# |d| from the score's bank and logistic nodes in place of |tanh| nodes, and the fold's product moved behind R's, in an attention and expert kernel

## What is computed

```python
def _L0_conv_ref(x, Wf, bf, Wg, bg, Wh, bh, Wv, bv, gamma):    # self-attention in each image
    s = jnp.einsum('bnd,bmd->bnm', xf @ Wf + bf, xf @ Wg + bg)
    o = gamma * (jax.nn.softmax(s, axis=-1) @ (xf @ Wh + bh)) @ Wv + bv + xf

def step(carry, ht):                                           # _L1_attn_ref, scanned over 256 tokens
    H_prev, H_prev_tilde = carry                               # the last 5 tokens and outputs
    temp = jnp.tanh(H_prev @ W1 + (ht @ W2)[:, None, :] + H_prev_tilde @ W3)
    w_t = jax.nn.softmax(temp @ v, axis=1)
    ht_hat = jnp.sum(H_prev_tilde * w_t, axis=1)
    ht_tilde = ht + jax.nn.relu(ht_hat)
    ...                                                        # both windows move on by one

t = _to_tokens(x)
t = t + _L1_attn_ref(_ln_t(t), v, W1, W2, W3)
t = t + _L1_ffn_ref(_ln_t(t), Wr, br, W1, b1, W2, b2)          # top 2 of 8 experts, Gelu
```

## Time and profile before

| | |
|---|---|
| runs (us) | 582.26, 577.89, 580.36, median 580.36 |
| the profiled execution | 582.32 us, of which its span 580.40 |
| busy | PE 557.9 us (96%), PEld 446.0 (77%), DVE 413.3 (71%), ACT 354.0 (61%), POOL 47.4 (8%) |

### The profile page before, as it was taken

The page is one execution under the profiler, slowest core; times in us unless marked ns, Lnnn a source line. Parts: engine busy times, 40 slices in busy tenths (PEclk is TensorE's granted clock), DMA queues, the critical chain, the costliest instruction groups (busy, mean ns, idle before and its releaser), DMA issues. The chain is left out here.

```text
span 580.4 us, 19441 instructions
## 1 busy us (share of the span) xinstructions
PE 557.9 (96%) x6331; PEld 446.0 (77%) x6331; DVE 413.3 (71%) x2867; ACT 354.0 (61%) x1440; POOL 47.4 (8%) x101
## 2 busy tenths in 40 slices
PE   6999879999999999999999999999999999999987
PEld 3555436778888888888888888888888888888875
DVE  2456555777777878787877787878787877777763
ACT  2335645556666666666666666666666666666654
POOL 1000000010101010101010101010101010101010
PEclk9555569999999999999999999999999999999999
DMA  8000000000000000000000000000000000000000
GB/s 228 17 2 1 0 0 3 2 3 2 3 6 3 6 3 7 3 7 3 6 3 6 3 6 3 7 3 7 2 6 3 6 3 7 2 7 3 8 2 10
DMA packets 7507, 5.84 MB, mean 10 GB/s; under 512 B 1216, under 2 KB 6896, under 8 KB 7408
## 3 DMA queue, kind: packets, MB, share of 16 engines
q1 hardware_dynamic: 6784, 4.57, 2.8%
q10 hardware_dynamic: 528, 0.03, 0.1%
q0 software_dynamic: 96, 0.00, 0.0%
HBM read 3.55 MB, written 1.05 MB: 8 GB/s over the span
## 5 line engine op out<-in xcount | busy, mean ns | idle before, releaser
L470 ACT ACTIVATE th<-bank 128x32 f32<-128x32 f32 x255 | 51.3, 201 | 145.4 <-PE bank L696 145.4
L938 DVE TENSOR_TENSOR_SCAN CC<-th,DE 128x16 f32<-128x16 f32 x510 | 115.3, 226 | 0.5 <-issue 0.5
L728 PE MATMUL bank<-f,hid 128*128 128x128 f32 x512 | 112.9, 302 | 1.0 <-ACT hid L492 0.6
L497 ACT ACTIVATE GF<-Z,cst 64x32 f32<-64x32 f32 x255 | 105.4, 413 | 11.7 <-DVE Z L989 2.5
L942 DVE SCALAR_TENSOR_TENSOR DE<-CC,yh 128x40 f32<-128x40 f32 x509 | 81.9, 203 | 27.2 <-DVE yh L1005 0.5
L938 DVE TENSOR_TENSOR_SCAN C<-th,DE 128x16 f16<-128x16 f32 x255 | 49.3, 193 | 73.0 <-ACT th L470 68.3
L633 PE MATMUL bank<-xnT,f1p 128*128 128x128 f16 x1024 | 99.2, 219 | 0.2 <-ACT hid L492 0.2
L696 PE MATMUL bank<-Tf,v 128*128 128x32 f32 x510 | 99.3, 277 | 0.0
L685 PE MATMUL bank<-Tf,nv 128*128 128x32 f32 x510 | 98.9, 276 | 0.0
L492 ACT ACTIVATE hid<-bank,b1T 128x128 f32<-128x128 f32 x256 | 94.4, 369 | 5.7 <-PE bank L633 4.8
L694 PE MATMUL bank<-GF,cst 128*128 128x32 f32 x510 | 95.3, 269 | 0.0
(11 more groups left out here) (135 smaller groups left out, 827.3 us busy)
## 6 DMA issues: line engine op xcount, KB each, us to landing
x_tok<-in_x_dram SPq DMA_DIRECT2D x4, 256.0 KB, 4.3
f<-in_L_ffn_W_dram SPq DMA_DIRECT2D x1, 1024.0 KB
out_dram<-acc SPq DMA_DIRECT2D x16, 64.0 KB
w<-in_L_attn_W_dram SPq DMA_DIRECT2D x3, 64.0 KB, 3.9
cst<-shape_constants_dram SPq DMA_DIRECT2D x1, 148.5 KB, 2.5
wfg<-in_L_conv_Wf_dram ACTq DMA_DIRECT2D x1, 8.0 KB, 2.3
wfg<-in_L_conv_Wg_dram ACTq DMA_DIRECT2D x1, 8.0 KB, 2.3
bhc<-in_L_conv_bh_dram POOLq DMA_DIRECT2D x1, 0.1 KB, 3.4
```

The source lines that it names most:

```text
L470: act.activation(th[p][:, 0:W4, 1], psS[p][:, 0:W4], ACT.Tanh, bias=-K0 / 2, scale=0.5 / WS).then_inc(th_ready, 1)
L497: act.activation(GF[p][0:NODES, :], Z[p][0:NODES, :], ACT.Tanh, bias=half_nodes, scale=half_nodes).then_inc(f_ready, 1)
L728: mm = pe.matmul(psO[e % 2][:, 0:D], hid[u % 2][:, :], f2[:, u, :], start=(half == 0), stop=(half == HH - 1))
L938: return dve.tensor_tensor_scan(flat[0], flat[1], flat[2], 0.0, ALU.mult, ALU.add)
```

## The change

The correction is now formed from other nodes: log(1+exp(-x)) is a sum of logistic functions, and ACT takes tanh((|d| + t)/2) for each node t. Every eighth node is a constant one, whose weight balances those ahead of it. |d| comes from the bank itself, by an Abs on ACT into a new tile `A`, behind the Relu in ACT's queue; the tanh of nodes follows behind a wait on it, ahead of the other work of the step. It covers 24 columns, no longer 32 (the last 8 stay as `g_init` has put them), its scale is a constant, and only its bias is a value for each row. `Z` and its VectorE instruction go, so do the bias of `th` and of Relu and the semaphores `z_ready` and `g_ready`. On TensorE the fold goes directly behind R2's products, and the filler that stood behind `h_products` goes.

```diff
--- before.py
+++ after.py
@@ -61,32 +61,46 @@
 
 NODES = 64
 LIN = NODES
-NODE_H = (np.log(22.0) - np.log(1e-8)) / (NODES - 1)
+RUN = 8
+SPREAD = 19.0
 
 
 def node_constants():
 
-    a = np.exp(np.log(1e-8) + NODE_H * np.arange(NODES)).astype(np.float32)
-    h = np.float32(NODE_H)
-    return a, h, float(np.sum(float(h) * np.tanh(a.astype(np.float64))))
+    u = np.linspace(-SPREAD, SPREAD, NODES - NODES // RUN)
+    h = u[1] - u[0]
+    t = np.full(NODES, 80.0)
+    w = np.zeros(NODES, np.float32)
+    owed = 0.0
+    at = 0
+    for j in range(NODES):
+        if j % RUN < RUN - 1:
+            t[j] = np.log1p(np.exp(u[at]))
+            w[j] = WS * h / 2 / (1 + np.exp(-u[at]))
+            owed += float(w[j])
+            at += 1
+        else:
+            w[j] = -owed
+            owed += float(w[j])
+    return t, w
 
 
 def shape_constants():
 
-    a, h, _ = node_constants()
+    t, w = node_constants()
     c = np.zeros((P, 2 * P + 1 + E + W4), np.float32)
     c[:, 0:P] = np.eye(P)
     c[LIN, P:2 * P] = -1.0
-    c[0:NODES, P:2 * P] = h * np.float32(WS)
-    c[0:NODES, 2 * P] = a / 2
+    c[0:NODES, P:2 * P] = w[:, None]
+    c[0:NODES, 2 * P] = t / 2
     c[:, 2 * P + 1:2 * P + 1 + E] = np.arange(E)
     for j in range(OLD):
         c[:, 2 * P + 1 + E + j * B:2 * P + 1 + E + (j + 1) * B] = np.log(OLD - j) * WS
+    c[0:NODES, 2 * P + 1 + E:] = 1.0
     return c
 
 
 def build(nc, x, Wf, bf, Wg, bg, Wh, bh, Wv, bv, gamma, v, W1, W2, W3, Wr, br, F1, b1, F2, b2, consts, out):
-    K0 = node_constants()[2]
     x_tok_dram = x.rearrange("b h w c -> b (h w) c").rearrange("b (u p) c -> p (b u) c", p=P)
     out_dram = out.rearrange("b h w c -> b (h w) c")
 
@@ -168,7 +182,7 @@
         Tf = pair("Tf", [P, W5])
         th = pair("th", [P, W5, 2])
         GF = pair("GF", [P, W4])
-        Z = pair("Z", [P, W4])
+        A = pair("A", [NODES, W4 - B])
         DE = pair("DE", [P, W5, 2])
         CC = pair("CC", [P, W5 + B, 2])
 
@@ -237,10 +251,9 @@
         score_ready = sem("score_ready")
         th_ready = sem("th_ready")
         crit_ready = sem("crit_ready")
-        z_ready = sem("z_ready")
+        a_ready = sem("a_ready")
         r1_ready = sem("r1_ready")
         r2_ready = sem("r2_ready")
-        g_ready = sem("g_ready")
         f_ready = sem("f_ready")
         y_ready = sem("y_ready")
         yh_ready = sem("yh_ready")
@@ -443,9 +456,6 @@
             act.wait_ge(projected, 1)
             tanh_of_item(1)
 
-            act.wait_ge(z_ready, 1)
-            act.wait_ge(g_ready, 1)
-            act.activation(GF[1][0:NODES, :], Z[1][0:NODES, :], ACT.Tanh, bias=half_nodes, scale=half_nodes).then_inc(f_ready, 1)
 
             def tile(k, base, steps, chain):
                 for i in range(steps):
@@ -467,10 +477,13 @@
                             act.activation(ul[:, :], dl[:, :], ACT.Tanh, scale=0.5).then_inc(ul_done, TS)
                     if chain and not first:
                         act.wait_ge(score_ready, n)
-                        act.activation(th[p][:, 0:W4, 1], psS[p][:, 0:W4], ACT.Tanh, bias=-K0 / 2, scale=0.5 / WS
+                        act.activation(th[p][:, 0:W4, 1], psS[p][:, 0:W4], ACT.Tanh, scale=0.5 / WS
                                        ).then_inc(th_ready, 1)
-                        act.activation(GF[p][:, 0:W4 - B], psS[p][:, B:W4], ACT.Relu, bias=K0 * WS, scale=-1.0
-                                       ).then_inc(g_ready, 1)
+                        act.activation(GF[p][:, 0:W4 - B], psS[p][:, B:W4], ACT.Relu, scale=-1.0)
+                        act.activation(A[p][:, :], psS[p][0:NODES, B:W4], ACT.Abs).then_inc(a_ready, 1)
+                        act.wait_ge(a_ready, n)
+                        act.activation(GF[p][0:NODES, 0:W4 - B], A[p][:, :], ACT.Tanh, bias=half_nodes, scale=0.5 / WS
+                                       ).then_inc(f_ready, 1)
                     if early and i == 1:
 
                         act.wait_ge(stats, jb + TS)
@@ -491,10 +504,6 @@
                         act.wait_ge(up_ps, jb + u + 1)
                         act.activation(hid[u % 2][:, :], hidden(k, u), ACT.Gelu, bias=b1T[:, u:u + 1], scale=1 / WS
                                        ).then_inc(gelu_done, 1)
-                    if chain and not first:
-                        act.wait_ge(z_ready, n + 1)
-                        act.wait_ge(g_ready, n + 1)
-                        act.activation(GF[p][0:NODES, :], Z[p][0:NODES, :], ACT.Tanh, bias=half_nodes, scale=half_nodes).then_inc(f_ready, 1)
 
             over_tiles(tile)
 
@@ -686,12 +695,10 @@
 
                         pe.wait_ge(r2_ready, n)
                         product(in5(psA[p][:, 0:W5]), w3w, relu, False, True, ALL_PRODUCTS[2:]).then_inc(projected, 1)
-                        h_products(k, i, q)
-                        keep_busy(psS[p], 256, 1)
-
-                        pe.wait_ge(g_ready, n)
                         pe.wait_ge(f_ready, n)
                         pe.matmul(psS[p][:, 0:W4], fold_w, GF[1 - p][:, :], start=False, stop=False)
+                        h_products(k, i, q)
+
                         pe.wait_ge(tf_ready, n + 1)
                         pe.matmul(psS[p][:, 0:W4], v32[:, :], Tf[p][:, 0:W4], start=False, stop=True).then_inc(score_ready, 1)
                     if first:
@@ -832,8 +839,6 @@
                     dve.memset(th[q][:, :, 0], 0.0).then_inc(init, 1)
                     dve.memset(th[q][:, W4:W5, 1], 1.0).then_inc(init, 1)
                     dve.memset(CC[q][:, :, :], 0.0).then_inc(init, 1)
-                    dve.memset(GF[q][:, :], 0.0).then_inc(init, 1)
-                    dve.memset(Z[q][:, :], 1.0).then_inc(z_ready if q == 1 else init, 1)
                 dve.memset(C16[0][:, :, :], 0.0).then_inc(r1_ready, 1)
                 dve.memset(R2[0][:, :], 0.0).then_inc(r2_ready, 1)
 
@@ -866,9 +871,10 @@
                 if i == B + 1:
                     initial_state()
 
-            dve.wait_ge(init, 9)
-
-            dve.tensor_copy(GF[1][:, :], g_init).then_inc(g_ready, 1)
+            dve.wait_ge(init, 6)
+
+            dve.tensor_copy(GF[0][:, :], g_init).then_inc(init, 1)
+            dve.tensor_copy(GF[1][:, :], g_init).then_inc(f_ready, 1)
             dve.wait_ge(ht_done, B)
 
             dve.tensor_copy(ybuf[0][:, 0, :], hT[:, 0, :]).then_inc(y_ready, 1)
@@ -986,8 +992,6 @@
                         mix(p, 0, B, C16[q]).then_inc(r1_ready, 1)
                         mix(p, 0, B).then_inc(crit_ready, 1)
 
-                        dve.scalar_tensor_tensor(Z[p][:, 0:W4 - B], th[p][:, B:W4, 1], -1.0,
-                                                 th[p][:, B:W4, 1], ALU.mult, ALU.max).then_inc(z_ready, 1)
 
                         attended = CC[p][:, 0:B, 1]
                         dve.wait_ge(crit_ready, n)
```

## The result

The changed kernel took 756.28 us (median of 4 runs, 730.14 to 783.67) against 581.31 (577.89 to 583.29): it is slower. The ratio, taken from its two faster runs (730.14 and 733.69), is 1.260, 95% interval 1.248 to 1.272; the other two took 778.86 and 783.67, the last being the profiled one. All four show the same fault, at different lengths: their mean granted clocks are 0.636, 0.620, 0.567 and 0.552, against 0.941 in the profile before.

A forecast was written before the change was run, and what follows sets the result against it. The bound was a chain of 255 attention steps, v's product waiting for `Tf` and the fold queued ahead; 240 steps at 0.095 us gave 22.8 us, 580.36 to 558 us, range 550 to 575.

The forecast's parts named there:

- The filler goes: TensorE, behind the hp products: removing the 256-column filler was counted on the way to the fold, no longer to v.
- Its other duty, the clock: The filler's role in holding TensorE's clock, left to a rival: clock falls, kernel slower; chance 0.07.
- The fillers of four stay where there is no expert work: Argument against a clock fall: TensorE keeps these fillers in steps without expert work; no size given.
- the step shrinks with its work: Argument against a clock fall: less TensorE work, but also a shorter step, 1.72 instead of 1.82 us.
- The rival's price: Cost of a clock fall on TensorE's path pieces: +0.45 us a step, 115 us if held throughout (672); chance 0.07.
- The mixture: Clock low in part of the chain's steps: slower than before from a fifth of them; a quarter gives 586 us.
- The sum of the gain: Attention chain: 240 steps at 0.095 us each, 22.8 us, giving 558 us, 3.9% faster.
- The steps with `b2`: 15 chain steps with the b2 product, where v already waited for `Tf` alone: no gain.
- The fold's input: Tanh of nodes on ACT: ends 0.67 to 0.89 us after `th`, before R's products, so the fold waits for nothing.
- its 0.055 a step: Estimated gain per step in us if |d| stayed on VectorE: 13 us in all instead of 22.8.
- rival 2: ACT becomes the bound, Gelu between tanh and `Tf`: 0.01 to 0.14 us more in 240 steps, say 592 us; chance 0.06.
- Rival 1: Fold on TensorE ready late: only 0.035 to 0.055 us a step gained, 8 to 13 us, say 570; chance 0.07.

The follow-up runs named there:

- experiment 1: The kernel before with only its 256-column filler behind the hp products taken out: 783.4 us, ratio 1.36.
- experiment 2: The changed kernel with the 256-column filler put back behind the hp products, ahead of v's product: 557.1 us, ratio 0.964.
- experiment 6: The changed kernel with TensorE's queue as before (hp products, filler of 256, fold, v), so only the nodes changed: 552.6 us, ratio 0.958.
- experiment 7: The kernel before, old nodes, with only the fold and its two waits moved directly behind R's products, filler kept: 767.9 us.
- 9: The kernel before with its 256-column filler behind the hp products only from tile 4 on: 782.8 us, ratio 1.357.
- 10: The kernel before with its filler only from tile 4 on, and 48 fillers of 256 columns in that tile's first step: 619.6 us, ratio 1.074.
- 11: The changed kernel run again as it is: 783.63 and 725.46 us.
- experiment 8: The changed kernel with the 256-column filler behind the hp products only from tile 4 on: 559.8 us, ratio 0.971.
- experiment 3: The changed kernel with a filler of 128 columns behind the hp products: 551.9 us, ratio 0.959.
- experiment 4: The changed kernel with a 256-column filler behind the expert's products, only in steps with expert work: 559.3 us, ratio 0.965.

## Why the prediction was wrong

**The step that failed is "The filler goes", with "Its other duty, the clock" left to a rival of 0.07.** The rival named the mechanism, and it happened: the clock fell. "The fillers of four stay where there is no expert work" was no cover, since the fall came where the expert work replaces them; "the step shrinks with its work" was none either: it fell near 129 us with the shorter step (the profile after) and with the old one (experiment 1). That the level before was a plain 1.00 says nothing of how far it is from falling, and I read it as distance. Experiments 1 and 2 make the cause certain: out in the old kernel, 1.36; back in the new one, 0.964.

**The rival's price was too low as well.** Said: 0.45 us a step, from the two stretches of TensorE that lay on the path. Measured, in an ordinary step: 2.63 - 1.73 = 0.90, and the chain took 670.7 us against 444.9 with the clock held. At the low level TensorE's other work, the expert's and the hp products, is no longer hidden, and TensorE is the bound from one `th` to the next. Scaling the path's own pieces misses what is pushed onto the path. The mixture ("slower than before as soon as a fifth of the steps run so") was wrong in kind for both profiled runs: the level wasn't lost for a while and regained, it fell once and stayed down to the chain's end.

**The sum of the gain was right, its cause half wrong.** Step 1.725 read, 1.72 said; 22.6 us in the chain, 22.8 said; with the clock held 552 to 560, 558 said. The steps with `b2`, 15 of them, gave nothing, as said: 2.04 us before and in experiment 2. But I put the gain down to the fold's place and kept the readiness of its input as a condition. Experiments 6 and 7 turn that around: the new nodes, with the input earlier, bring 0.958 alone, the place alone makes a step of 2.00. The prediction noted that the fold loaded 0.12 after its input's end, and still made the filler the other half of the wait. The earlier trace rows can't decide between the two, as the filler's load had ended 0.09 before the fold's began. The two experiments can: behind a filler the fold's load needs 0.02, and behind its input it takes 0.12 again when no filler is there. The sum came out right because the change made the input early as well; that part was luck.

**The other steps.** The fold's input: the tanh ended at 0.69 (0.67 to 0.89 said, and the low end taken). Abs started at 0.17 and took 0.18, as Relu does; the tanh itself 0.31, a little over the 0.28. The rule of the Trainium skill that would keep |d| on VectorE (page "ScalarE: Activation LUTs", Rules for kernel authors) was not tried in a run, so its 0.055 a step stays an estimate; Abs on ACT at any rate held nothing up. Gelu behind the tanh delayed nobody at the high level: `Tf` started at 1.03 in a step without a Gelu (115.04), and in experiment 6 at 1.02, with the Gelu (L505, 302.01) ended at 0.94 (1.02 said), so rival 2 did not happen. `R` still started 0.55 after `th`: Z's going gave nothing, as said. No step stretched behind `xn`. Rival 1 did not happen.

**What stays open.** What exactly tips the level, and why the low one stays. Shown is that it held with 64, 128 or 256 columns more and failed at some point without, that it can hold for three tiles without, and that experiment 7 lost it with every filler in place. One regularity stands in the traces: in all five in which it fell with the filler missing (after, 1, 9, 10, 11) it fell 0.5 to 3.1 us behind the experts' first product (at 126.9 us in the profile after), so at the passage from the steps with four fillers to those with expert work; experiment 8 passed the same place unharmed, and in experiment 7 the fall came 27 us ahead of it. That chance enters through where the steps lie in time is only my guess.

## What to carry to other kernels

A filler on TensorE that looks idle in the timeline may be what holds the clock; before taking one out, treat it as a change of its own, with its own chance, and leave it in when the rest is moved. A level of 1.00 shows no margin, and a fall of the clock is not to be priced by stretching the path: ask whether TensorE's whole queue still fits into the step at half speed, for if it doesn't, every step gets longer by what is left over, and here the clock then stayed low although TensorE was never idle. When an instruction stands behind two things, the gaps in one timeline (0.12 and 0.09 here) may not tell which one it waits for: take away one of them in a run, and then the other.

## What the hardware showed that I had not expected

The low level persists at a fully busy TensorE: 500.00 of 500 us busy and the clock at 0.50 (experiment 9), while the same instructions in the kernel before hold 1.00 with 19.59 of 20 us busy; 48 fillers of 256 columns in a row lifted it (experiment 10). The Trainium skill, "TensorE: Matmul & The Clock Gate", Part 1, has it that activity releases the throttle; the burst agrees, but the busy share of the profile doesn't tell that activity. The fold's weight load was issued 0.02 us after the filler's, though the filler has 256 columns (experiment 6).

And the time ahead of the chain varies, with the clock: the first `th` starts at 86.0 us in experiment 3 and at 93.4 in experiment 8, with the same code up to there. The first layer ran at these granted clocks (experiment 3, then 8):

```profile
50.00:80.00 30.00, 22.36 (x71) 10.74 (x71) 16.66 (x53) 15.67 (x29) 3.22 (x5) 0.69 0.00 0
```

```profile
50.00:80.00 30.00, 25.13 (x67) 12.31 (x65) 17.37 (x51) 17.05 (x34) 2.76 (x4) 0.50 0.00 0
```

In one execution the clock is up for part of the first layer, in the other it is not. The difference of 7.4 us is as much as the medians of the good versions lie apart, and their chains, that of experiment 4 aside, agree within 0.6 us. So the scatter between them comes from ahead of the chain and says nothing of the change.
